# Flamingo block on one core: the first batch's projections as a program of their own, with 24 turns of a tile of ones ahead of them

## The reference, cut to what matters

```python
q = layernorm(x) @ Wq.T; k = ctx @ Wk.T; v = ctx @ Wv.T          # 8 x 512/1601 x 256, 16 heads of 16
attn = softmax(einsum('bhnc,bhlc->bhnl', q * 256**-0.5, k), axis=2)
attn = attn / sum(attn, axis=-1)
x = x + tanh(g_xattn) * (einsum('bhnl,bhlc->bhnc', attn, v) @ Wo.T)
x = x + tanh(g_ffn) * experts(layernorm(x))                      # 2 of 8 experts a row, 256 -> 1024 -> 256
```

## Time and profile before

| what | value |
|---|---|
| median of three runs | 1856.92 us |
| the profiled execution | 1859.11 us |
| its span, first to last instruction | 1857.4 us |
| PE busy | 1679.9 us, 90% |
| DVE busy | 1410.9 us, 76% |
| ACT busy | 1282.1 us, 69% |
| POOL busy | 555.3 us, 30% |

### The profile page before, as it was taken

The page is one execution under the profiler, slowest core; times in us unless marked ns, Lnnn a source line. Parts: engine busy times, 40 slices in busy tenths (PEclk is TensorE's granted clock), DMA queues, the critical chain, the costliest instruction groups (busy, mean ns, idle before and its releaser), DMA issues.

```text
span 1857.4 us, 31398 instructions
## 1 busy us (share of the span) xinstructions
PE 1679.9 (90%) x9888; PEld 890.5 (48%) x9888; DVE 1410.9 (76%) x2273; ACT 1282.1 (69%) x3634; POOL 555.3 (30%) x833
## 2 busy tenths in 40 slices
PE   5789999999989999999998998886499999999997
PEld 3223333333323333333332332212499999999997
DVE  1599999999999999999999999995444444444442
ACT  1699999999999999999999999993111111111111
POOL 5142152234225135234322522212222222222222
PEclk8899999999999999999999999998699999999999
DMA  5914612711731651371172163206422222222222
GB/s 153 232 33 129 161 39 80 195 52 61 189 88 45 155 151 39 101 199 46 54 200 73 57 155 84 80 23 222 144 37 37 37 36 35 37 37 37 37 34 29
DMA packets 124933, 168.64 MB, mean 91 GB/s; under 512 B 14320, under 2 KB 102256, under 8 KB 124816
## 3 DMA queue, kind: packets, MB, share of 16 engines
q1 hardware_dynamic: 102064, 136.77, 27.5%
q0 software_dynamic: 13344, 17.90, 5.9%
q10 hardware_dynamic: 9408, 12.58, 1.9%
HBM read 117.96 MB, written 49.24 MB: 90 GB/s over the span
## 4 chain that ended last, share of the span: by engine, by line
PE 36%; ACT 30%; DVE 20%; issue 7%; POOL 3%; DMA 2%; ACTq 1%; SPq 0%; POOLq 0%; DVEq 0%
ACT w_all L673 28%; DVE negmax L824 14%; PE scores L1116 13%; PE scores L1129 12%; PE scores L563 3%; PE acc L576 3%; DVE resid L725 1%; PE spare L506 1%; POOL routed_rows L949 1%; ACT w_all L629 1%; PE spare L496 1%; DMA w_all<-in_ctx_t 1%; DMA out<-row_t,gate_token 1%; PE spare L1106 1%; DVE rz L810 1%
## 5 line engine op out<-in xcount | busy, mean ns | idle before, releaser
L673 ACT ACTIVATE w_all<-scores,negmax 128x512 f32<-128x512 f32 (+1 forms) x1664 | 1127.8, 753 | 33.9 <-DVE negmax L824 27.0
L824 DVE TENSOR_REDUCE negmax<-scores 128x2 f32<-128x1024 f32 (+1 forms) x832 | 1002.4, 1216 | 82.5 <-PE scores L563 73.2
L563 PE MATMUL scores<-q_stack,w_all 128*128 128x512 bf16 (+1 forms) x1664 | 502.6, 384 | 53.6 <-ACT w_all L673 51.5
L673 ACT ACTIVATION_READ_ACCUMULATOR w_all<-scores,negmax 128x1 f32 (+1 forms) x1664 | 452.6, 272 | 0.0
L576 PE MATMUL acc<-w_all,vz 128*32 128x512 f32 (+1 forms) x3328 | 443.2, 605 | 4.1 <-POOL vz L958 3.9
L1155 ACT ACTIVATE projections<-scores 128x512 f32<-128x512 f32 x142 | 84.8, 598 | 453.5 <-PE scores L1116 442.6
L563 PEld LDWEIGHTS scores<-q_stack,w_all 128*128 128x128 bf16 (+1 forms) x1664 | 115.4, 99 | 531.2 <-ACT w_all L673 399.4
L958 POOL TENSOR_TENSOR vz<-w_all,rz 128x68 f32<-128x68 f32 (+1 forms) x416 | 125.3, 301 | 807.1 <-DVE rz L810 788.0
L1116 PEld LDWEIGHTS scores<-row_t,q_stack 128*128 128x128 f32 x2272 | 267.1, 193 | 7.1 <-issue 2.0
L1116 PE MATMUL scores<-row_t,q_stack 128*128 128x128 f32 x2272 | 268.3, 277 | 1.8 <-DVE row_t L1182 1.8
L1129 PE MATMUL scores<-room,projections 128*128 128x256 f32 x1136 | 256.8, 379 | 0.0
(11 more groups left out here) (136 smaller groups left out, 1035.2 us busy)
## 6 DMA issues: line engine op xcount, KB each, us to landing
w_all<-k_parts SPq DMA_DIRECT2D x256, 200.1 KB, 3.5
q_stack<-q_parts SPq DMA_DIRECT2D x256, 64.0 KB, 3.3
w_all<-in_ctx_t SPq DMA_DIRECT2D x8, 1601.0 KB
k_parts<-parts SPq DMA_DIRECT2D x42, 300.0 KB, 2.9
w_all<-in_w ACTq DMA_DIRECT2D x12, 1024.0 KB, 11.9
parts<-routed SPq DMA_DIRECT2D x71, 129.0 KB
q_parts<-parts SPq DMA_DIRECT2D x14, 384.0 KB, 3.3
k_parts<-parts SPq DMA_DIRECT2D x14, 300.8 KB, 3.5
```

Of the source, the lines that this page charges most:

```text
L563: mm = pe.matmul(scores[0:r, 2 * (u % SLOTS) + j % 2, :], k_stack[:, g, j, lt * P:lt * P + r], q_stack[:, g, j, :], start=True, stop=True)
L673: e = act.activation(probs[0:r, s % RING, j, :], scores[0:r, 2 * (u % SLOTS) + j % 2, :], ACT.Exp, bias=negmax[0:r, u % 4, j % 2:j % 2 + 1 ...
L824: dve.tensor_reduce(negmax[0:r, u % 4, :], scores[0:r, 2 * (u % SLOTS):2 * (u % SLOTS) + 2, :], AX.X, ALU.max, negate=True).then_inc(negma ...
```

## The change

The first batch gets a program of its own, `first()`, on every engine, ahead of the iterations. Iteration -1 is gone, and so are `FIRST_FILL_AT`, `two_banks` and `parts_of`.

- PE turns `ones` 24 times into `acc`, then makes 15 pieces (`EARLY`) through all eight PSUM banks: k 0, k 1, the two turns of x, k 2, q 0, k 3 to 7, q 1, and v 0 to 2.
- The values v 3 to 6 of batch 0 (`own_v`) become fills of batch 0 itself, at steps 1, 3, 5 and 6. Batch 0 has a table of its own, where k 0 of batch 1 stands at step 11 instead of 1.
- The context of batch 0 comes in two halves with a semaphore each. Every weight has a semaphore of its own. ACT issues the loads of `wq` and of the gates.
- DVE normalises x, and makes residual, middle and low part of all pieces.
- SP loads the k blocks of a group's stack, POOL stores q 0 and loads the q blocks of groups 0 and 1. The context of batch 1 is loaded once `own_v` 6 is taken.
- ACT waits in steps 0 to 3 only for those stores whose parts lie under the `probs` that it writes.
- Later batches are as before but for the counts.

```diff
+FIRST_BATCH_FILL_AT = {
+    1: ("cur", "own_v", 3), 3: ("cur", "own_v", 4), 5: ("cur", "own_v", 5), 6: ("cur", "own_v", 6),
+    11: ("next", "k", 0), 13: ("next", "k", 1), 15: ("next", "k", 2), 16: ("cur", "o_turn", 0),
+    18: ("next", "k", 3), 20: ("next", "k", 4), 22: ("next", "k", 5), 24: ("next", "k", 6), 26: ("next", "k", 7),
...
+EARLY = (("k", 0), ("k", 1), ("x_turn", 0), ("x_turn", 1), ("k", 2), ("q", 0), ("k", 3), ("k", 4), ("k", 5), ("k", 6),
+         ("k", 7), ("q", 1), ("v", 0), ("v", 1), ("v", 2))
+BANKS_EARLY = 8
+WARM_TURNS = 24
...
-    run(Iteration(-1, tail=False, cur=False))
     run(Iteration(0, tail=False))
...
+        def first():     # SP
             sp.dma_start(x_in[:, :, :], x_rows[0]).then_inc(x_loaded, 16)
             sp.dma_start(wk_sb[:, :, :], wk_t.rearrange("(k p) n -> p k n", p=P)).then_inc(wk_in, 16)
+            for half, cols in enumerate((slice(0, halfway), slice(halfway, L))):
+                sp.dma_start(ctx_sb[:, :, cols], ctx_rows[0][:, :, cols]).then_inc(early_ctx[half], 16)
+            for w_sb, w, w_in in ((wv_sb, wv_t, wv_in), (wo_sb, wo_t, wo_in), (router_sb, router_t, wo_in)):
+                sp.dma_start(w_sb[:, :, :], w.rearrange("(k p) n -> p k n", p=P)).then_inc(w_in, 16)
+            for i in range(KCHUNK):
+                store_early(sp, "k", i)
+            stored_early(sp, *(("k", i) for i in range(KCHUNK)))
+            for blk in range(BLOCKS):
+                load_k_block(sp, 0, 0, blk)
+            for i in range(KCHUNK, 2 * KCHUNK):
+                store_early(sp, "k", i)
+            store_early(sp, "q", 1)
+            for blk in range(BLOCKS):
+                load_k_block(sp, 0, 1, blk)
+            sp.wait_ge(early_copied, KC)
+            sp.dma_start(x_in[:, :, :], x_rows[1]).then_inc(x_loaded, 16)
+            stored_early(sp, ("q", 1), *(("k", i) for i in range(KCHUNK, 2 * KCHUNK)))
             load_stacks(0, 2)
...
+        def first():     # PE
+            pe.wait_ge(constants, 1)
+            for _ in range(WARM_TURNS):
+                pe.transpose(acc[:, 0:P], ones[:, :], ident[:, :])
+            for n, (name, i) in enumerate(EARLY):
...
+        def first():     # DVE
...
+            for at, (name, i) in enumerate(EARLY_SPLIT):
...
+                dve.scalar_tensor_tensor(out=resid[:, at % 2, 0:cols], in0=early_bank(n)[:, 0:cols],
+                                         scalar=D ** -0.5 if name == "q" else 1.0, in1=high,
+                                         op0=ALU.mult, op1=ALU.subtract).then_inc(early_split, 1)
+                dve.wait_ge(early_split, at + 1)
+                dve.tensor_copy(middle, resid[:, at % 2, 0:cols]).then_inc(middle_ready, 1)
+                dve.wait_ge(middle_ready, at + 1)
+                dve.tensor_tensor(low, resid[:, at % 2, 0:cols], middle, ALU.subtract).then_inc(parts_ready, 1)
...
+        def first():     # POOL
+            pool.wait_ge(mv_ready, NT)
+            one_over_deviation(mv1, rstd1, rstd_step, 0)
+            store_early(pool, "q", 0)
+            stored_early(pool, ("q", 0))
+            for blk in range(BLOCKS):
+                load_q_block(pool, early_q_in, 0, 0, blk)
+            for blk in range(BLOCKS):
+                load_q_block(pool, early_q_in, 0, 1, blk)
+            pool.dma_start(out[TOKENS:TOKENS + P, :], pad_row[:, 0:D]).then_inc(rows_out, 16)
+            pool.wait_ge(early_copied, len(EARLY_COPIED))
```

More of the change, by code:

```diff
@@ L102, in __init__ @@
         has = {"tail": tail, "cur": cur, "next": nxt}
-        self.first = isinstance(b, int) and b < 0
-        self.ahead = nxt and not (isinstance(b, int) and b + 2 >= B)
-        self.table = FIRST_FILL_AT if self.first else FILL_AT
+        self.ahead = nxt and not (b + 2 >= B)
+        self.table = FIRST_BATCH_FILL_AT if b == 0 else FILL_AT
         order = [self.table[s] for s in sorted(self.table) if has[self.table[s][0]]]
@@ L110, in __init__ @@
         full = len(FILL_AT)
[L111 to L118, removed]
+        ahead = sum(1 for kind, _, _ in FILL_AT.values() if kind == "next")
+        self.base = 0 if b == 0 else len(FIRST_BATCH_FILL_AT) + (b - 1) * full - (ahead if b == B else 0)
     def fill(self, s):
@@ L282, in attention_and_routing @@
     row_f = sb("row_f", [P, NBLK])
[L285 to L291, removed]
+    early_parts = under(w2_all, 0, [CHUNKS, 3, N], BF16)
+    EARLY_PART = 3 * N // 2
     scores = ctx.enter_context(nc.psum_tensor("scores", [P, 2 * SLOTS, N], F32))
@@ L295, in attention_and_routing, with early_bank @@
     spare = ctx.enter_context(nc.psum_tensor("spare", [P, N], F32))
-    weights_in = sem("weights_in")
-    wk_in = sem("wk_in")
+    def early_bank(n):
+        return (*(scores[:, i, :] for i in range(2 * SLOTS)), spare[:, :], acc[:, :])[n % BANKS_EARLY]
+    wq_in, wk_in, wv_in, wo_in = (sem(f"{w}_in") for w in ("wq", "wk", "wv", "wo"))
     gates_in = sem("gates_in")
@@ L315, in attention_and_routing @@
     fill_taken = sem("fill_taken")
+    early_ctx = [sem(f"early_ctx_{half}") for half in range(2)]
+    early_q_in = [sem(f"early_q_in_{g}") for g in range(2)]
+    early_ready = sem("early_ready")
+    early_split = sem("early_split")
+    early_copied = sem("early_copied")
+    early_stored = [sem(f"early_stored_{at}") for at in range(CHUNKS)]
     high_ready = sem("high_ready")
@@ L413, in run @@
             b = it.b
-            if it.first:
-                first(it)
-                return
+            if b == 0:
+                sp.wait_ge(fill_taken, it.made("own_v", VF - 1))
+                sp.dma_start(ctx_sb[:, :, :], ctx_rows[1]).then_inc(ctx_loaded, 16)
             if it.cur:
@@ L710, in pick @@
             yield
+        def first():
+            dve.wait_ge(x_loaded, 16)
+            for t in range(NT):
+                dve.bn_stats(stats1[:, t, :], x_in[:, t, :]).then_inc(stats_done, 1)
+            dve.wait_ge(stats_done, NT)
+            for t in range(NT):
+                dve.bn_aggr(mv1[:, t, :], stats1[:, t, :]).then_inc(mv_ready, 1)
+            dve.wait_ge(rstd_step, 2)
+            for t in range(NT):
+                row = dve.tensor_scalar(x_in[:, t, :], x_in[:, t, :], mv1[:, t, 0:1], rstd1[:, 1, t:t + 1],
+                                        ALU.subtract, ALU.mult)
+                if t % 2:
+                    row.then_inc(xn_ready, 1)
+            for at, (name, i) in enumerate(EARLY_SPLIT):
+                n = EARLY.index((name, i))
+                cols = columns(name, i)
+                high, middle, low = (early_parts[:, at, part, 0:cols] for part in range(3))
+                dve.wait_ge(high_ready, at + 1)
+                dve.scalar_tensor_tensor(out=resid[:, at % 2, 0:cols], in0=early_bank(n)[:, 0:cols],
[5 more added lines that the diff above has]
+                dve.tensor_tensor(low, resid[:, at % 2, 0:cols], middle, ALU.subtract).then_inc(parts_ready, 1)
         def take(it, name, i):
@@ L835, in run @@
                     f = it.fill(s)
-                    if f and f[0] not in ("v", "x_turn") and p == (f[0] in ("q", "k")):
+                    if f and f[0] not in ("v", "own_v", "x_turn") and p == (f[0] in ("q", "k")):
                         take(it, *f)
@@ L877, in run @@
                         in_turn(placing, place_steps)
+        first()
+        dve.wait_ge(constants, 1)
         over_batches(dve, run)
```

262 lines of the change are left out of this document (162 added, 100 removed).

## The result

The changed kernel takes 1843.88 us at the median of four runs (1838.86 to 1845.21), against 1857.13 for the kernel before: a ratio of 0.9924, interval 0.9909 to 0.994. That is 13.2 us faster and clear of 0.2%, but 15.2 us short of the 28.4 us forecast, and above the range, which ended at 1839.0. The profiled execution took 1844.35 us (span 1842.6).

The account below looks back on a forecast made before the run. ScalarE's exponentials were taken to bound the kernel behind the prologue; 30.7 us sooner less 1.8 and 0.5 gave 28.4 us, so 1828.5 us at the median, range 1824.5 to 1839.

Parts of the forecast that it names:

- What bounds the kernel: Whole kernel: ScalarE's exponentials set the attention's pace from about 67 us, so the prologue is what there is to win.
- First loads: Prologue start: earlier issue saves 0.9 us, waiting for half the context 2.3, so k 0 starts at 9.1 us.
- Turns of ones: TensorE before k 0: 24 turns end by 9.1 us, k 0 runs at 2.4 GHz; without them 1.5 us more.
- stays at 1.2 GHz: Rival, TensorE in the prologue: low clock doubles its 20.9 us, gain only 10 us, 1847 us; chance 0.07.
- Splits: VectorE in the prologue: middle part 0.35 us, 1.65 us a k piece, 2.0 a q piece, k 3 ends at 20.3.
- Stores and stacks: Prologue DMAs: k 0 to 3 stored at 23.1 us, last blocks landed by 32.6, first scores at 33.0 against 54.06.
- a better bound beside it: DMA engines in the prologue: 2.1 MB at 211 GB/s from 23.1 us lands at 36, three us later.
- POOL's queue: Rival, POOL's DMA issues beside VectorE's splits: 1.7 us each instead of 0.95, gain 16.5, 1840.4 us; chance 0.12.
- Into the attention: After the first scores: exponentials at 34.9 us, ScalarE's second unit at 36.2 against 66.92, 30.7 us sooner.
- What comes back: Batch 0: four takes of v cost ScalarE 1.8 us, waiting for batch 1's context 0.5 us.

Follow-up runs that it names:

- Run 5: Changed kernel with 44 turns of ones instead of 24: 1841.41 us, ratio 0.9919.
- run 3: Changed kernel with POOL issuing group 1's q blocks only once group 0's k blocks have landed: 1845.62 us, ratio 0.993.
- run 7: Changed kernel with the q blocks of groups 0 and 1 back in SP's queue, POOL only storing q 0: 1847.83 us, ratio 0.9951.
- run 9: run 6 with 44 turns, group 0's k stack in two halves, and stores of k 4 to 7 ahead of the second halves: 1833.80 us.
- Run 1: Changed kernel with group 2's stack blocks issued behind the load of batch 1's context instead of ahead: 1841.42 us, ratio 0.9918.
- run 2: Changed kernel with the blocks of groups 2 and 3 issued only once batch 1's context has landed: 1843.65 us, ratio 0.9924.
- run 6: Changed kernel with group 2's blocks behind batch 1's context and, in batch 0, group 3's behind the stores of k 0 to 7: 1836.74 us.
- Run 4: Changed kernel with no turns of ones instead of 24: 1844.49 us, ratio 0.9929.
- run 10: run 6 with 44 turns of ones and nothing else: 1834.68 us, ratio 0.9882.

## Why the prediction was wrong

**What bounds the kernel: right.** ScalarE holds the pace behind the prologue before and after, and what the prologue gives, less what comes back, reaches the end: 14.7 us by the account above, 14.8 between the two profiled executions, 13.2 between the medians.

**First loads: nearly right.** k 0 started at 10.06, forecast 9.1, bounds 8 and 11.4. The first half of the context, issued at 1.85, landed at 9.93.

**Turns of ones: wrong.** The sum took them for out of the way by 9.1 and k 0 for 2.4 GHz. They were out of the way too soon, at 7.67, and k 0 and k 1 took 4.62 us against 2.92 with 44 turns. That is 1.7 us; the rival "stays at 1.2 GHz" fell otherwise, since from about 13.8 us until TensorE waited for the stacks the granted clock was 1.00.

**Splits: right, a little dear.** A middle part took 0.370 us (taken 0.35), and k pieces followed one another every 1.50 us (taken 1.65). k 3 was ready at 22.67 instead of 20.3, for the late start and the clock.

**Stores and stacks: wrong; the first scores came 6.3 us late.** 2.4 of them were there before any store: k 3 was ready that much late. Run 5 gets back 2.7 of the 6.3 with the clock. The store took 3.93 us for 2.8. The last k block was issued at 31.32, 3.7 us later than forecast, and landed in 7.96 for 3.6: at 39.27 instead of 31.2, 8.1 us late, of which 1.8 were slack in the forecast, whose scores were at 33.0. Both prices came from rows where the engines weren't full: their share was 0.45 from 18.6 to 24.5 us, with those stores, and 0.71 from 34.3 to 44.5 with those blocks. The forecast had a better bound beside it (211 GB/s, first scores at 36) and set it aside because one row showed 3.6 us; k 0 to 3 were in DRAM at 26.63 instead of 23.1, and with these 3.5 us that bound comes to 39.5, against 39.32 measured. It also counted only q and k of group 0, while group 1's q blocks and the stores of k 4 to 7 were in the same engines: runs 3, 7 and 9 each move the scores or the blocks by moving such bytes.

**POOL's queue: the rival fell.** 16 issues took 8.11 us, 0.51 each, with VectorE's splits beside them; I had taken 0.95 and feared 1.7. TensorE's waits from 30 to 110 us have none for `vz`. The rule that the prediction set beside it (the Trainium skill, "SBUF — State Buffer", "DVE blocks DMA": no descriptors from GpSimd during VectorE's two-port copies) doesn't show in these issues: they run from 0.508 to 0.598 us, beside VectorE's casts as after them. Whether the casts take both ports, and whether descriptors were late behind the issue, no row here tells.

**Into the attention: 1.7 us off.** The second unit came 4.9 us behind the first scores instead of 3.2. The chain names it: TensorE filled a piece of v (40.36, 1.71 us) between the two units' scores, and it did so slowly: after 7 us of waiting for the stacks the granted clock was 0.50 from 36 to 40 us, and the first unit's scores took 1.03 us, 0.59 in the earlier trace rows. The same four matmuls of v took 1.03 us from 49.52 on. In that form the prediction's rival of the low clock came true for a stretch.

**What comes back: the step that failed.** I charged the context 0.5 us, from a load of 8.3 us. SP's queue around that load, in the kernel before:

```profile
48.42 1.07 SPq L365 DMA_DIRECT2D q_parts<-w_all  x1
54.66 0.37 SPq L390 DMA_DIRECT2D w_all<-in_ctx_t  x1
56.10 0.54 SPq L377 DMA_DIRECT2D q_stack<-q_parts  x1
```

It had blocks behind it, but nothing had been issued for 5.2 us ahead of it. In the changed kernel it stands behind group 2's 16 blocks and ahead of group 3's, all of them moved forward by the very gain that was forecast, and took 13.75 us; ScalarE's waits after the second unit came to 6.4. Run 1 shows that with these blocks behind it the load takes 6.7 us, run 2 that alone it takes 6.23, run 6 that with the order mended 7.1 us come back. The prediction asked what the queue of SP saves; it never listed what the queue held between 43 and 75 us at the new times. "No wait of TensorE on the context above 1 us" was the test that it set, and the trace has 5.0.

The sizes add up: 6.3 for the first scores, 1.7 for the second unit and 5.9 for the context, less 0.2 for the takes of v, are 13.7 us, and the profiled execution was forecast at 1830.7 and took 1844.35. The medians lie 15.4 apart, because the profiled execution before lay 2.2 us above the median that the forecast used, and the one after 0.5. The chances were too sure for the same reason. The range reached 1839.0, for a slow POOL, and had the DMA engines in it only with three us. The rivals were all engines and queues; none was a transfer that comes late because everything ahead of it came early.

**What stays open.** Why the changed kernel's runs spread over 6 to 9 us and those of run 6 over 1.3 was not tried. Run 4's trace shows a part of it: its SP queue is ordered as in the changed kernel, its profiled execution took 1839.70 us, and the context landed sooner.

```profile
59.98 11.40 DMA w_all<-in_ctx_t
```

ScalarE's hole is 3.38 us there instead of 5.74, and its last instruction of the eighth batch's attention comes 3.1 us sooner than in the changed kernel's trace. Another 1.8 us lie between that instruction and the first block of experts (53.7 us, against 55.5), and nothing here says why. Nor was it tried whether fewer and larger blocks would load a stack faster.

## What to carry to other kernels

When a prologue gets shorter, lay out the bytes of every DMA at its new time, and add up what stands ahead of each load that has a deadline: a landing time read from a row where the DMA engines weren't full is no price for one where they are. In this kernel a second queue bought little once the engines were full; the order did, each transfer by when it is wanted, and moving one load behind another is only done when what then stands behind both has been looked at too. Turns that are to raise TensorE's clock must last until close to the real work: here an idle time of 0.96 us behind them cost nothing (run 10), and one of 2.39 us the whole gain.

## What was not expected of the hardware

A direct DMA of 64 KB costs GpSimd 0.51 us to issue, whether or not VectorE runs its casts beside it; the earlier trace rows had 0.78 for the cheapest, and that same DMA (`pad_row`) takes 0.57 here. With the engines full of stacks' blocks and x, from 45 to 60 us, they moved 222 GB/s (211 in the earlier trace rows), while the loads of the first microseconds reach more:

```profile
7.00:10.00 3.00, 0.67 (x6) 0.43 (x4) 1.37 (x9) 0.61 (x1) 1.29 (x2) 1.00 0.89 330
```

So a block stands for more engine time than its bytes say. The clock after the turns wasn't the same every time: in run 2, with the same 24 turns, they took 5.38 us, the idle time was 1.93, and k 0 and k 1 took 2.92 at a granted clock of 1.00. In the other six traces with 24 turns TensorE idled 2.39 to 2.77 us, and the two pieces were slow; with 44 turns it idled at most 0.96 us, and they took 2.92 in all four. So run 2's trace has its first scores sooner for a reason that isn't its edit. And without turns the granted clock reads 1.00 from 10 to 13.6 us although the two pieces take 4.39 us, so there that column doesn't show why they were slow. The turns began in the same way: in run 5 there were 6 of them from 4 to 5 us and 12 from 8 to 9, at a granted clock of 1.00 in both.
